# A sequence model's ternary weights and its modulation chain, set up in one block

## What is computed

```python
def _bitlinear(x, w, nw, b=None):
    xn = x * rsqrt(mean(square(x), -1) + 1e-08) * nw
    xq = clip(round(xn * s), -128, 127) / s          # s = 127 / max(|xn|, 1e-5), per row
    wq = _weight_quant(w)                            # ternary, one scale a matrix
    y = xq @ wq.T
    return y if b is None else y + b

h = _bitlinear(silu(c), wa0, na0)
gate, y = split(_bitlinear(h, wa1, na1), 2)
h = _bitlinear(silu(gate) * y, wa2, na2)
h = _rmsnorm(_bitlinear(h, wa3, na3, ba3), wr, 1e-06)
params = _bitlinear(h, wa4, na4, ba4)
```

## Time and profile before

| | us |
|---|---|
| median of 3 runs | 2297.39 (2296.23 to 2297.98) |
| the profiled execution | 2293.55 |
| its span, first to last instruction | 2291.7 |
| VectorE's last pass over the weights ends | 110.75 |
| `params` is complete, its store is issued | 176.22 |
| `layers01` begins | 179.34 |

### The profile page before, as it was taken

How to read it: one execution, slowest core, us unless ns; L and a number is a source line. 1 busy time by engine, 2 the same in 40 slices (tenths; PEclk the granted TensorE clock), 3 DMA queues, 4 the chain that set the end, 5 groups by cost and what they waited for, 6 DMA issues and landing times. The chain is left out here.

```text
span 2291.7 us, 26057 instructions
## 1 busy us (share of the span) xinstructions
PE 1849.1 (81%) x8698; PEld 1099.3 (48%) x8698; DVE 1408.0 (61%) x2885; ACT 1092.8 (48%) x2109; POOL 600.7 (26%) x780
## 2 busy tenths in 40 slices
PE   0033457999898999758999999999999975799998
PEld 0011235566566667523244454545454355476756
DVE  3844588888878873357867687776766214333331
ACT  5102466776777763123575657666665710112121
POOL 0013675566566441300000010101001010232332
PEclk9985679999999999877899999999999986899999
DMA  8023000000000000221120202112020002000000
GB/s 318 4 74 96 17 14 8 10 17 17 1 17 12 4 8 3 84 56 25 35 58 4 58 4 60 35 28 58 4 58 4 6 4 89 0 13 16 10 19 19
DMA packets 87989, 78.36 MB, mean 34 GB/s; under 512 B 9632, under 2 KB 81768, under 8 KB 87600
## 3 DMA queue, kind: packets, MB, share of 16 engines
q1 hardware_dynamic: 87856, 76.70, 12.3%
HBM read 46.85 MB, written 4.27 MB: 22 GB/s over the span
## 5 line engine op out<-in xcount | busy, mean ns | idle before, releaser
L1651 DVE TENSOR_REDUCE l_small<-l_psum 128x1 f32<-128x512 f32 x512 | 330.0, 685 | 136.0 <-PE l_psum L1598 130.8
L1410 ACT ACTIVATE l_prob<-l_psum 128x512 f32<-128x512 f32 x512 | 286.4, 596 | 228.8 <-PE l_psum L1468 225.6
L1598 PE MATMUL l_psum<-l_kT,l_qT 96*128 96x512 bf16 x512 | 193.3, 414 | 25.7 <-DMA l_kT<-l_early 12.1
L1468 PE MATMUL l_psum<-l_qT,l_kT 99*128 99x512 bf16 x512 | 175.2, 386 | 16.2 <-ACT l_prob L1410 14.3
L1394 POOL TENSOR_TENSOR k_x_res<-k_x_res,l_add 128x256 f32<-128x256 f32 x32 | 23.3, 727 | 469.5 <-DVE l_add L1695 469.5
L1477 PE MATMUL l_psum<-l_prob,l_v 128*32 128x512 f32 x1024 | 138.1, 612 | 0.2
L1542 PE MATMUL l_psum<-l_w,l_gu 128*128 128x256 f32 x512 | 135.1, 393 | 0.7 <-ACT l_gu L1426 0.7
L1598 PEld LDWEIGHTS l_psum<-l_kT,l_qT 96*128 96x128 bf16 x512 | 49.6, 98 | 171.6 <-DVE l_small L1651 117.4
L94 PE MATMUL l_psum<-l_turned_over,l_w 128*128 128x512 f32 x256 | 120.7, 598 | 4.2 <-ACT l_gu L1426 4.2
L94 PE MATMUL l_psum<-l_hT,l_w 128*128 128x512 f32 x256 | 116.8, 606 | 8.6 <-ACT l_hT L2005 8.6
L931 PE MATMUL l_psum<-l_w_f,l_gu 128*128 128x256 f32 x512 | 120.5, 382 | 0.8 <-ACT l_gu L771 0.8
(11 more groups left out here) (369 smaller groups left out, 4005.5 us busy)
## 6 DMA issues: line engine op xcount, KB each, us to landing
qw_own<-in_L_cond_wa SPq DMA_DIRECT2D x1, 9216.0 KB, 34.7
l_qT<-l_early SPq DMA_DIRECT2D x32, 192.0 KB, 3.6
l_kT<-l_early SPq DMA_DIRECT2D x32, 192.0 KB, 3.3
k_x_res<-in_x SPq DMA_DIRECT2D x1, 4096.0 KB
l_w<-in_L_cond_W SPq DMA_DIRECT2D x4, 1024.0 KB, 10.2
l_qT<-l_early SPq DMA_DIRECT2D x32, 128.0 KB, 3.2
l_kT<-l_early SPq DMA_DIRECT2D x32, 128.0 KB, 3.1
out<-k_x_res SPq DMA_DIRECT2D x8, 512.0 KB, 2.9
```

The source lines that it names most:

```text
L1410: act.activation(prob[:, s % 2, j, :], psum[:, 2 + n % 2, :], ACT.Exp, scale=float(HD) ** -0.5).then_inc(exp_ready.sem, 1)
L1468: pe.matmul(psum[:, 2 + n % 2, :], kT[e % 2][:, head, tok(s % T)], qT[e % 2][:, head, :], start=True, stop=True).then_inc(st_ready.sem, 1)
L1598: pe.matmul(psum[:, n % 2, :], qT[e % 2][0:SROWS, n // T, tok(n % T)], kT[e % 2][0:SROWS, n // T, :], start=True, stop=True).then_inc(s_re ...
L1651: dve.tensor_reduce(mx[:, n % T, n // T:n // T + 1], psum[:, n % 2, :], AX.X, ALU.max).then_inc(max_ready.sem, 1)
```

## The change

Both functions go, and `setup` does their work in one block.

- The condition arrives turned over (`condT`), and the chain keeps features on 128 partitions and samples along the row: `h` is 128 x (k x 8). Its vectors come as rows and are turned over once on TensorE. Sums over features go through TensorE with ones, the largest value through a turn-over, a diagonal and another product (`squares`, `largest`, `spread`). The products of `wa0` to `wa3` have the weight stationary, 128 x 128, and 8 columns moving (`product`); that of `wa4` has the samples stationary as before, and follows its weight piece by piece.
- The scale pass of the weights goes to ScalarE (`scaled`, fp32 in place, pieces of 1536). VectorE rounds into bf16 (`whole`) and clips in bf16 in place (`clipped`). `wm1`'s absolute values are summed by VectorE. ScalarE's elementwise result of `absolute` goes to SBUF in bf16.
- Each main weight has a place of its own (`raw_main`), `wa4` comes in six transfers, and `x` is loaded once `wa0` to `wa3` are rounded.
- The orders of the engines are written out; here they are, with the added lines that matter, indented less than in the file:

```diff
+PIECE = OUT6
+LOAD4 = 2
+COND_N = ("na0", "na1", "na2", "na3", "na4")
+VECTORS = (("na0", KD), ("na1", KD), ("na2", KA), ("na3", KD), ("na4", K6), ("wr", K6), ("ba3", K6))
+WM1 = len(COND_W) + 4
...
+def setup(nc, io, main, mean, ident, mod0, x_res, x_loaded):
+    groups = COND_W + MAIN_W
...
+        raw2, raw4, raw_main = sb("raw2", [P, size[2]]), sb("raw4", [P, size[4]]), sb("raw_main", [P, sum(size[5:])])
+        first4 = sb("first4", [P, PIECE], BF16)
+        tern = [sb("t_" + name, [P, k * n], BF16) for name, k, n in COND_W[:4]]
...
+        def codes(i, a, z):
+            if i == 4:
+                return first4[:] if a == 0 else raw4[:, a - PIECE:a].bitcast(BF16)[:, 0:PIECE]
+            return (tern[i] if i < 4 else main[i - 5])[:, a:z]
...
+    sp.dma_start(by_k(h, KD), io["condT"].rearrange("(k p) b -> p k b", p=P)).then_inc(cond_loaded, 16)
+    weight(0)
+    a = 0
+    for name, k in VECTORS:
+        sp.dma_start(rows[a:a + k, :], io["L0_cond_" + name].rearrange("(k p) -> k p", p=P)).then_inc(rows_loaded, 16)
+        a += k
+    for i in (1, 2, 3):
+        weight(i)
+    for c in range(0, K6, LOAD4):
+        sp.dma_start(raw4[:, c * PIECE:(c + LOAD4) * PIECE].rearrange("p (k n) -> p k n", k=LOAD4),
+                     io["L0_cond_wa4"][c * P:(c + LOAD4) * P, :].rearrange("(k p) n -> p k n", p=P)).then_inc(loaded4[c // LOAD4], 16)
+    sp.dma_start(ba4[:], row_of(io["L0_cond_ba4"]).to_broadcast([B, OUT6])).then_inc(ba4_loaded, 16)
+    for i in range(5, len(groups)):
+        weight(i)
+    sp.wait_ge(rounded, piece_number(4, 0))
+    sp.dma_start(x_res[:].rearrange("p (n d) -> p n d", d=D), io["x"].rearrange("b (t p) d -> p (b t) d", p=P)).then_inc(x_loaded, 16)
+    sp.wait_ge(params_ready, 3)
...
+    for n in range(len(COND_W) + 1):
+        pool.wait_ge(ms_ready, n + 1)
+        gp.tensor_tensor(rms[:], ms[:], half[:], ALU.pow).then_inc(rms_ready, 1)
...
+            ac.activation(junk[:, 0:z - a], raw[i][:, a:z], ACT.Abs, accum_out=parts[:, i, j:j + 1]).then_inc(abs_summed, 1)
...
+    def scaled(i):
+        act.wait_ge(inv_ready, i + 1)
+        for a, z in pieces_of(i):
+            ac.activation(raw[i][:, a:z], raw[i][:, a:z], ACT.Copy, scale=inv[:, i:i + 1]).then_inc(scaled_up, 1)
+    act.wait_ge(cond_loaded, 16)
+    ac.activation(h[:, 0:KD * B], h[:, 0:KD * B], ACT.Silu).then_inc(silu_ready, 1)
+    absolute(0)
+    scaled(0)
+    absolute(1)
+    absolute(2)
+    scaled(1)
+    scaled(2)
+    absolute(3)
+    act.wait_ge(h_ready, 2)
+    ac.activation(h[:, 0:KA * B], h[:, 0:KA * B], ACT.Silu).then_inc(gate_ready, 1)
+    scaled(3)
+    absolute(4)
+    scaled(4)
+    for i in range(5, 9):
+        absolute(i)
+    for i in range(5, 9):
+        scaled(i)
+    absolute(10)
+    scaled(9)
+    scaled(10)
...
+        pe.wait_ge(q_ready, i + 1)
+        pe.wait_ge(code_ready, piece_number(i + 1, 0))
+        if i == 0:
+            pe.wait_ge(cols_ready, 1)
+        for c in range(n // P):
+            last = mm(nc, ps_t[:, c * B:(c + 1) * B], [(tern[i][:, m * n + c * P:m * n + (c + 1) * P], q[:, m * B:(m + 1) * B]) for m in range(k)])
+        last.then_inc(y_ready, 1)
...
+    total(0)
+    squares(0)
+    largest(0)
+    spread(0)
+    product(0)
+    squares(1)
+    largest(1)
+    total(1)
+    spread(1)
+    total(2)
+    product(1)
+    squares(2)
+    largest(2)
+    total(3)
+    spread(2)
+    product(2)
+    squares(3)
+    largest(3)
+    spread(3)
+    product(3)
+    squares(4)
+    squares(5)
+    largest(4)
+    spread(4)
+    total(4)
+    pe.wait_ge(q_ready, 5)
+    for c in range(K6):
+        pe.wait_ge(code_ready, piece_number(4, c) + 1)
+        w4 = codes(4, c * PIECE, (c + 1) * PIECE)
+        for a in range(3):
+            last = nc.tensor.matmul(ps_y[0:B, a, :], q[:, c * B:(c + 1) * B], w4[:, a * 512:(a + 1) * 512], start=(c == 0), stop=(c == K6 - 1))
+    last.then_inc(y_ready, 1)
+    for i in range(5, len(groups)):
+        total(i)
...
+    def whole(i, j):
+        a, z = pieces_of(i)[j]
+        dve.wait_ge(scaled_up, piece_number(i, j) + 1)
+        if i == 4 and j:
+            dve.wait_ge(rounded, piece_number(i, j))
+        V.tensor_scalar(codes(i, a, z), raw[i][:, a:z], ROUND, ROUND, ALU.add, ALU.subtract).then_inc(rounded, 1)
+    def clipped(i, j):
+        a, z = pieces_of(i)[j]
+        dve.wait_ge(rounded, piece_number(i, j) + 1)
+        V.tensor_scalar(codes(i, a, z), codes(i, a, z), 1.0, -1.0, ALU.min, ALU.max).then_inc(code_ready, 1)
+    def ternary(i):
+        n = len(pieces_of(i))
+        whole(i, 0)
+        for j in range(1, n):
+            whole(i, j)
+            clipped(i, j - 1)
+        clipped(i, n - 1)
...
+    def squared(k, n):
+        V.tensor_tensor(sq[:, 0:k * B], h[:, 0:k * B], h[:, 0:k * B], ALU.mult).then_inc(sq_ready, 1)
+        dve.wait_ge(sq_ready, n + 1)
+        V.tensor_reduce(sqk[:], over_k(sq, k), AX.X, ALU.add).then_inc(sqk_ready, 1)
+    def mean_square(k, n, eps):
+        dve.wait_ge(summed, n + 1)
+        V.tensor_scalar(ms[:], ps_sum[:, 0:B], 1.0 / (k * P), eps, ALU.mult, ALU.add).then_inc(ms_ready, 1)
+    def front(i, n):
+        k = width[i]
+        squared(k, n)
+        V.tensor_tensor(by_k(xn, k), by_k(h, k), col(COND_N[i]), ALU.mult).then_inc(xn_ready, 1)
+        dve.wait_ge(xn_ready, i + 1)
+        V.tensor_reduce(pmax[:], over_k(xn, k), AX.X, ALU.max, apply_absolute_value=True).then_inc(pmax_ready, 1)
+    def peak(i, n):
+        dve.wait_ge(max_turned, i + 1)
+        V.tensor_reduce(top[:], ps_max[0:B, 0:P], AX.X, ALU.max).then_inc(top_ready, 1)
+        dve.wait_ge(top_ready, i + 1)
+        V.tensor_scalar(diag[:], ident[0:B, 0:B], top[:], None, ALU.mult).then_inc(diag_ready, 1)
+        mean_square(width[i], n, 1e-8)
+    def quantised(i, n):
+        k = width[i]
+        step = Chain(dve, scale_step, i, 3)
+        dve.wait_ge(max_ready, i + 1)
+        dve.wait_ge(rms_ready, n + 1)
+        step.link(V.tensor_tensor(s4[:], ps_all[:, 0:B], rms[:], ALU.mult))
+        step.link(V.tensor_scalar(s4[:], s4[:], 1e-5, 1.0 / 127.0, ALU.max, ALU.mult))
+        step.link(V.reciprocal(s6[:], s4[:]))
+        V.tensor_tensor(s6[:], s6[:], rms[:], ALU.mult).then_inc(s6_ready, 1)
+        step.close()
+        dve.wait_ge(s6_ready, i + 1)
+        step = Chain(dve, qv_step, i, 2)
+        step.link(V.tensor_tensor(by_k(qv, k), by_k(xn, k), every(s6, k), ALU.mult))
+        step.link(V.tensor_scalar(qv[:, 0:k * B], qv[:, 0:k * B], ROUND, None, ALU.add))
+        V.tensor_scalar(q[:, 0:k * B], qv[:, 0:k * B], ROUND, None, ALU.subtract).then_inc(q_ready, 1)
+        step.close()
+        V.tensor_scalar(s5[:], s4[:], mean[:, i:i + 1], None, ALU.mult).then_inc(s5_ready, 1)
+    def taken(i):
+        k = groups[i][2] // P
+        dve.wait_ge(s5_ready, i + 1)
         dve.wait_ge(y_ready, i + 1)
+        V.tensor_tensor(by_k(h, k), by_k(ps_t, k), every(s5, k), ALU.mult).then_inc(h_ready, 1)
+        dve.wait_ge(h_ready, i + 1)
+    inverse(0)
+    dve.wait_ge(cols_turned, 1)
+    V.tensor_copy(cols[:], ps_t[:, 0:cols.shape[1]]).then_inc(cols_ready, 1)
+    dve.wait_ge(cols_ready, 1)
+    dve.wait_ge(silu_ready, 1)
+    front(0, 0)
+    ternary(0)
+    peak(0, 0)
+    quantised(0, 0)
+    taken(0)
+    front(1, 1)
+    inverse(1)
+    peak(1, 1)
+    quantised(1, 1)
+    inverse(2)
+    ternary(1)
+    taken(1)
+    ternary(2)
+    dve.wait_ge(gate_ready, 1)
+    step = Chain(dve, tail_step)
+    step.link(V.tensor_tensor(h[:, 0:KA * B], h[:, 0:KA * B], h[:, KA * B:2 * KA * B], ALU.mult))
+    front(2, 2)
+    inverse(3)
+    peak(2, 2)
+    quantised(2, 2)
+    whole(3, 0)
+    clipped(3, 0)
+    taken(2)
+    front(3, 3)
+    whole(3, 1)
+    clipped(3, 1)
+    peak(3, 3)
+    quantised(3, 3)
+    taken(3)
+    step.link(V.tensor_tensor(by_k(h, K6), by_k(h, K6), col("ba3"), ALU.add))
+    squared(K6, 4)
+    step.link(V.tensor_tensor(by_k(h, K6), by_k(h, K6), col("wr"), ALU.mult))
+    mean_square(K6, 4, 1e-6)
+    dve.wait_ge(rms_ready, 5)
+    step.link(V.tensor_tensor(by_k(h, K6), by_k(h, K6), every(rms, K6), ALU.mult))
+    front(4, 5)
+    peak(4, 5)
+    dve.wait_ge(ba4_loaded, 16)
+    for j in (1, 4):
+        V.tensor_scalar(ba4[:, j * D:(j + 1) * D], ba4[:, j * D:(j + 1) * D], 1.0, None, ALU.add).then_inc(ba4_step, 1)
+    inverse(4)
+    quantised(4, 5)
+    dve.wait_ge(s5_ready, 5)
+    V.tensor_tensor(own5[:], s5[0:B, :], ident[0:B, 0:B], ALU.mult).then_inc(own_step, 1)
+    dve.wait_ge(own_step, 1)
+    V.tensor_reduce(out_scale[:], own5[:], AX.X, ALU.add).then_inc(own_step, 1)
+    ternary(4)
+    dve.wait_ge(loaded[WM1], 16)
+    for j, (a, z) in enumerate(pieces_of(WM1)):
+        if j == 1:
+            dve.wait_ge(y_ready, 5)
+            dve.wait_ge(own_step, 2)
+            dve.wait_ge(ba4_step, 2)
+            for b in range(3):
+                V.scalar_tensor_tensor(out=params[:, b * 512:(b + 1) * 512], in0=ps_y[0:B, b, :], scalar=out_scale[:],
```

(48 more changed lines are left out.)

235 lines of the change are left out of this document (85 added, 150 removed).

## The result

| | median, us | ratio to before, 95% interval |
|---|---|---|
| before, 4 runs | 2296.81 | |
| changed, 4 runs | 2211.68 (2208.49 to 2213.81) | 0.963 (0.9613 to 0.9648) |

The change makes the kernel 3.7% faster. The profiled execution took 2210.04 us, with a span of 2208.3.

The account below looks back on a forecast made before the run. Bound: two serial blocks, one chain from engine to engine, no engine full. Walking ScalarE's list put `layers01` at 103.4 instead of 179.34, 75.9 us less: 2293.55 became 2217.6, plus 3.84 for the median, 2221.5; range 2208 to 2235.

Parts of the forecast that it names:

- Step 1: Start of setup: small rows land near 7.5 us, `wa1` is issued near 5.5 and lands at 12.3; ScalarE waits for it.
- Step 2: ScalarE sums `wa1` and `wa2` to 18.7 us, scales `wa1` to 22.3; inverse(2), behind quantised(1) on VectorE, comes at 23.1.
- Step 3: Gate's Silu waits for product(1), 28 matmuls of 8 columns at 0.12 us each (bounds 0.06 and 0.235): ready at 30.2.
- Step 4: Scaling `wa3` waits for inverse(3) until 34.8 us, ends at 37.8; ScalarE idled about 10 us, all for the chain.
- Steps 5 and 6: `wa4` on ScalarE: sums 19.8 us, to 57.6, chain hidden with some 1 us spare; mean, inverse 1.4, scaling 17.5, to 76.5.
- Steps 7 and 8: Tail: `params` 80.9 to 82.9 us, four inverses to 90.6, ScalarE idle 7; VectorE's last pieces end at 102.4.
- Step 9: Block's end and semaphore reset take 1.0 us, from the store's end plus some 2 us; `layers01` begins at 103.4.
- the fast rival: Setup: the chain doesn't hold ScalarE up, its 10 us of idling shrink; 2219, or 2211 if all went; chance 0.08.
- the forecast case's own range: Likeliest case, chance 0.69: 2214 to 2230 us, each unknown price at either end, plus 2 us for the clock's edge.
- the first: Setup: VectorE becomes the bound if `clipped` runs like the fp32 pass, 0.96 us; `layers01` near 110, time 2228; chance 0.12.
- The second: Setup: the chain doesn't hold ScalarE up if powers and small products are cheaper; 2219, at the extreme 2211; chance 0.08.
- The slower kernel: `layers01` and after run more at TensorE's lower clock; with 200 us more there, about 2320; chance 0.02.

Follow-up runs that it names:

- Run 6: Changed kernel with each 8-column block of the products of `wa0` to `wa3` computed four times: `layers01` begins 2.27 us later, median 2215.43 us.
- run 4: Changed kernel without modulation layers 0 to 3 and the norm, last product on constant inputs: `layers01` begins 2.69 us earlier, median 2206.08 us.
- run 8: Changed kernel with ScalarE summing `wm1` and `wm2` in the reordered tail, and `wa4`'s first two pieces before scaling `wa3`: `layers01` 7.44 us earlier, median 2205.11 us.
- run 3: Changed kernel with rounding kept in fp32 and the clip reading fp32, writing bf16: `layers01` begins 7.45 us later, median 2218.79 us.
- run 2: Changed kernel with the weights' scaling moved back to VectorE, ScalarE only summing: `layers01` begins 14.51 us later, median 2226.44 us.

## Why the prediction was right, and where its sizes were off

Right: that the modulation chain would be hidden nearly whole, ScalarE would set the pace, and VectorE would keep up. Its steps, forecast and measured (us):

| step | forecast | measured |
|---|---|---|
| 1: `wa1` landed | 12.3 | 11.29 |
| 2: inverse(2) ready | 23.1 | 21.43 |
| 3: the gate's Silu can start | 30.2 | 26.06 |
| 4: sums of `wa4` begin | 37.8 | 33.02 |
| 5: they end | 57.6 | 52.56 |
| 6: scaled | 76.5 | 71.5 |
| 7: ScalarE's idle time after that | 7 | 6.41 |
| 8: VectorE's last pass ends | 102.4 | 95.77 |
| 9: `layers01` begins | 103.4 | 96.85 |

- **Step 1.** `condT` was issued in 0.44 us, not in 1.20, and the seven rows in 2.45, not 3.0. `wa1` was issued 1.3 us earlier and landed 1.0 us earlier. The rows came at 5.5, not at 7.5.
- **Step 2.** From there to inverse(2) it took 10.1 us, not 10.8: 0.7 us.
- **Step 3** is the term that failed most: 0.12 us a matmul, bounds 0.06 to 0.235, measured 0.03. From inverse(2) to the gate it took 4.6 us, not 7.1: 2.5 us, all of it this price. It lies below my lower bound, since that came from a weight load of 0.10 and I allowed for only two side by side. Run 6 confirms the price. ScalarE was still summing `wa3` until 26.43, so the Silu itself held up nothing; product(1) counts because it stands on VectorE's list ahead of inverse(3).
- **Step 4.** From the gate to the sums of `wa4` it took 7.0 us, not 7.6. Its sentence that ScalarE idles "about 10 us", "all for the chain", was wrong twice. The steps' own times leave 7.4 us of idling between 12.3 and 37.8 (25.5 less 18.1 of work), and the 10 went on into the price of a rival. Measured, it idled 3.9 us between 11.29 and 33.02, and run 4 shows the chain's part, 2.7; the rest is the mean and its inverse, which stay without the chain and which run 8 covers with other work.
- **Steps 5 and 6** were right: 19.54 us of sums (forecast 19.8), a scaling each 1.467 us (1.46), the clip 0.55 (0.56). The spare time was 3.4 instead of 1 us, as the products were cheaper. The powers took 1.64, as in the earlier trace rows.
- **Steps 7 and 8.** VectorE did not have to wait for the last product after its first piece of `wm1`: `params` came 5.9 us earlier than forecast (75.0, not 80.9), where its pass over `wa4` had ended 5.0 earlier. That is 0.8 us; inverses in a row took 1.085 us, not 1.23: another 0.6.
- **Step 9.** The store's "some 2 us" had no row; the seam from VectorE's last pass to `layers01` took 1.1 us, as forecast.
- **The rest.** From my sum, 2221.5, to 2211.7 it is 9.8 us. 6.6 are the setup's, 0.9 lie in `layers01` and after, and the median of the runs stands 1.6 above the profiled execution, where I had added 3.84 from the kernel before: 2.2 us. That last part is no more than which execution was profiled.
- **How good the hit was.** Every step came out early, so hardly any error cancelled another. The range held the time because it reached down to the fast rival; the forecast case's own range did not.

Of the rivals, the first happened when it was made (run 3) at nearly its price. The second, that the chain doesn't hold ScalarE up, came half true, by the products and not by the powers. Its extreme, 2211, is the time that was measured, but not for its reason: run 4 shows that the chain still costs 2.7 us. That VectorE has the cheaper column for the scaling was weighed, and run 2 answers it. The slower kernel did not come: the granted clock was 0.61 and 0.94 in the two stretches above against 0.65 and 0.94, and `layers01` and the rest took 2111.5 against 2112.4 us, inside the scatter given at the end.

## What to carry to other kernels

Where two serial blocks leave all engines partly idle, price the overlap first: here it was 44 of 82 us; the quantising's new passes and order gave 20, the chain's layout 11, and having its small loads in early some 7. Balance a chain of elementwise passes by the sum on each engine, not by which engine does one pass faster. After such a change, read the new pacing engine's idle times in its own timeline: filling two of them gave 7.4 us more, by order and by moving one weight's sums to ScalarE.
